# Expert stage of a product-key layer: scatter before the hidden products, weighting on GpSimd, output matmuls three pairs behind

## The reference, cut to what matters

```
for each head h:
    s1, s2   = scores of the query of (t, h) with two sets of 64 keys
    v1, i1   = the 16 best of s1;   v2, i2 = the 16 best of s2
    scores   = the 16 best of all v1[a] + v2[b], with expert = i1[a] * 64 + i2[b]
for each chosen expert e, with its score w:
    hidden   = gelu(expert_down[e] . xn[t]) * relu(w)
    out[t]  += hidden * expert_up[e]
```

## Time and profile before

| | |
|---|---|
| median of 3 runs | 2386.52 us (2382.08 to 2389.36) |
| span of the profiled execution, first to last instruction | 2389.1 us |
| expert loop in it, from the first hidden matmul to the last addition to x | 633.1 to 1861.4 us |
| TensorE, VectorE, ScalarE, GpSimd busy, of the span | 79%, 70%, 28%, 19% |

### The profile page before, as it was taken

The page is one execution under the profiler, slowest core; times in us unless marked ns, Lnnn a source line. Parts: engine busy times, 40 slices in busy tenths (PEclk is TensorE's granted clock), DMA queues, the critical chain, the costliest instruction groups (busy, mean ns, idle before and its releaser), DMA issues. The chain is left out here.

```text
span 2389.1 us, 47903 instructions
## 1 busy us (share of the span) xinstructions
PE 1889.5 (79%) x17539; PEld 1539.2 (64%) x17539; DVE 1684.3 (70%) x6987; ACT 669.6 (28%) x1493; POOL 462.3 (19%) x667
## 2 busy tenths in 40 slices
PE   6595899996479788797787977978769699747995
PEld 3364688874468677686676866767658577544653
DVE  3433666645899999999999999999996477430112
ACT  1342355544222131121311213112120255421220
POOL 2002344330020201202112021120220311021111
PEclk8796899998789899898998988989888799858997
DMA  2232444413400000000000000000000233212434
GB/s 60 70 97 59 113 104 106 99 34 113 102 6 5 2 6 1 6 6 1 6 2 6 5 2 6 1 6 2 1 2 1 60 86 83 68 68 82 141 103 122
DMA packets 90420, 110.24 MB, mean 46 GB/s; under 512 B 27168, under 2 KB 79088, under 8 KB 89552
## 3 DMA queue, kind: packets, MB, share of 16 engines
q1 hardware_dynamic: 84672, 99.09, 15.8%
q0 software_dynamic: 3344, 6.53, 0.8%
q10 hardware_dynamic: 2176, 1.61, 0.2%
HBM read 69.84 MB, written 33.83 MB: 43 GB/s over the span
## 5 line engine op out<-in xcount | busy, mean ns | idle before, releaser
L1665 PE MATMUL peer_out_ps<-peer_g,peer_up 128*128 128x256 f32 (+1 forms) x1664 | 379.0, 393 | 85.1 <-issue 77.1
L1665 PEld LDWEIGHTS peer_out_ps<-peer_g,peer_up 128*128 128x128 f32 x1664 | 326.7, 203 | 133.8 <-issue 85.2
L1630 PE MATMUL peer_x_ps<-peer_xc,peer_dt 128*128 128x256 f32 (+1 forms) x1664 | 352.7, 373 | 19.6 <-DMA peer_up<-in_L_ffn_expert_up_dram 19.5
L1630 PEld LDWEIGHTS peer_x_ps<-peer_xc,peer_dt 128*128 128x128 f32 x1664 | 306.8, 191 | 60.3 <-issue 20.6
L1579 POOL TENSOR_TENSOR peer_g<-peer_g,peer_qt 128x512 f32<-128x512 f32 x96 | 153.0, 1636 | 796.0 <-ACT peer_qt L1790 796.0
L1768 ACT ACTIVATE peer_g<-peer_x_ps 128x512 f32<-128x512 f32 (+1 forms) x208 | 119.1, 573 | 637.1 <-PE peer_x_ps L1630 637.0
L1284 DVE TENSOR_REDUCE l_attn_mx<-l_attn_s_ps 98x4 f32<-98x392 f32 (+1 forms) x320 | 175.0, 560 | 142.7 <-PE l_attn_s_ps L1054 101.6
L1654 PE MATMUL peer_x_ps<-peer_oh_h,peer_oh_a 128*128 128x32 bf16 x3136 | 171.5, 181 | 111.2 <-DVE peer_oh_l L1995 95.6
L1654 PEld LDWEIGHTS peer_x_ps<-peer_oh_h,peer_oh_a 128*128 128x128 bf16 x3136 | 165.1, 99 | 128.5 <-DVE peer_oh_l L1995 63.5
L1988 DVE TENSOR_TENSOR peer_oh_a<-peer_a_t,peer_iota_f 128x8192 bf16<-128x8192 bf16 x49 | 216.6, 4421 | 1.3
L1205 ACT ACTIVATE l_attn_pt<-l_attn_st_ps 98x392 f32<-98x392 f32 x320 | 148.2, 492 | 147.1 <-PE l_attn_st_ps L1067 146.0
(11 more groups left out here) (325 smaller groups left out, 3460.4 us busy)
## 6 DMA issues: line engine op xcount, KB each, us to landing
moe_w<-in_L_ffn_w_dram SPq DMA_DIRECT2D x16, 1024.0 KB, 7.8
l_attn_pieces_q_dram<-l_attn_pieces_q SPq DMA_DIRECT2D x16, 294.0 KB, 3.9
l_attn_pieces_k_dram<-l_attn_pieces_k SPq DMA_DIRECT2D x16, 294.0 KB, 3.2
l_attn_stq<-l_attn_pieces_q_dram SPq DMA_DIRECT2D x16, 294.0 KB
l_attn_stk<-l_attn_pieces_k_dram SPq DMA_DIRECT2D x16, 294.0 KB
peer_g<-n_L_ffn_expert_down_dram SPq DMA_DIRECT2D x8, 512.0 KB
peer_up<-in_L_ffn_expert_up_dram SPq DMA_DIRECT2D x2, 2048.0 KB, 17.6
moe_expert_in<-l_blank SPq DMA_DIRECT2D x16, 197.5 KB
```

Of the source, the lines that this page charges most:

```text
L1630: mm = nc.tensor.matmul(x_ps[b][:, jj * CT:jj * CT + cols], dt[:, k, 2 * jp + jj, :], xc[p][:, k, 0:cols], start=(k == 0), stop=(k == KC - 1))
L1665: mm = nc.tensor.matmul(out_ps[:, m * CT:m * CT + cols], up[:, j, m * P:(m + 1) * P], g[:, j, 0:cols], start=(j == 0), stop=(j == J - 1))
```

## The change

The weights are scattered first, straight into `g`: ScalarE copies each quarter from PSUM to `g` (`scattered`). Only after all scatters of a chunk come the hidden pairs. ScalarE's gelu goes to `act_out`, two buffers in the place of `qt`, and GpSimd multiplies each pair into `g` (`weigh`). TensorE issues the output matmuls of a pair (`pair_out`) three pairs (LAG) after its hidden pair, and the turns of the next chunk after output pair 13 (TURN_AT). GpSimd runs `candidates` of the next chunk after its multiplies 5 and 11 and `index_steps` after the last. VectorE's multiplies are gone, and its addition to `x` of the chunk before (`add_out`, one instruction for each half of the features) stands behind the first one-hots. The second half of the output sums has moved to the bank of `sim_ps[1]`, so `queries` waits for the addition. One of the four halvings in `fold` adds neighbours in place of halves.

```diff
@@ -1398,7 +1397,7 @@
         qt = S.sb("qt", [P, 4, CT])
-        m_copy = [qt[:, 2 * p:2 * p + 2, :].rearrange("p m t -> p (m t)") for p in range(2)]
+        act_out = [qt[:, 2 * p:2 * p + 2, :] for p in range(2)]
         sc = [S.sb(f"sc{p}", [TT, G16, NK]) for p in range(NTILE)]
@@ -1427,14 +1426,15 @@
         sim_ps = [S.ps(f"sim{p}") for p in range(2)]
-        tr_ps, out_ps = S.ps("tr"), S.ps("out")
+        tr_ps = S.ps("tr")
+        out_ps = [S.ps("out"), sim_ps[1]]
@@ -1459,7 +1459,8 @@
         NPAIR = J // 2
-        EARLY = 10
+        LAG = 3
+        TURN_AT = NPAIR - 3
         JS = 8
@@ -1562,24 +1563,25 @@

-            def next_tables(n, tiles):
-
-                for t in range(len(tiles)):
-                    candidates(n, t)
-                index_steps(n)
-
-            next_tables(0, tile_rows(CT))
+            def weigh(n, jp, cols):
+
+                pool.wait_ge(gelu_done, NPAIR * n + jp + 1)
+                pair = g[:, 2 * jp:2 * jp + 2, 0:cols]
+                nc.gpsimd.tensor_tensor(pair, pair, act_out[jp % 2][:, :, 0:cols], ALU.mult).then_inc(g_done, 1)
+
+            for t in range(NTILE):
+                candidates(0, t)
+            index_steps(0)

             def chunk(n, p, now, then):
-
-                for hb in range(LATE, now // HT):
-                    for q in range(4):
-                        pool.wait_ge(m_copied, 4 * (NHB - LATE) * n + 4 * (hb - LATE) + q + 1)
-                        ts = slice(hb * HT + q * GT, hb * HT + (q + 1) * GT)
-                        nc.gpsimd.tensor_tensor(g[:, :, ts], g[:, :, ts], m_copy[q % 2].rearrange("p (t j) -> p j t", j=J),
-                                                ALU.mult).then_inc(g_done_late, 1)
+                tables = dict(zip((5, 11), range(len(tile_rows(then)))))
+                pool.wait_ge(m_copied, 4 * NHB * n + 4 * (now // HT))
+                for jp in range(NPAIR):
+                    weigh(n, jp, now)
+                    if jp in tables:
+                        candidates(n + 1, tables[jp])
                 if then > 0:
-                    next_tables(n + 1, tile_rows(then))
+                    index_steps(n + 1)
             chunks(pool, chunk)
@@ -1603,6 +1605,7 @@
                 wait(pe, sim_ready, NTILE * n)
+                wait(pe, x_done, n - 1)
                 for m in range(4):
@@ -1618,18 +1621,17 @@

-            def hidden(n, p, pairs, cols):
...
+            def hidden(n, p, jp, cols):
+                b = jp % 4
+                if jp < 4:
+                    pe.wait_ge(m_copied, 4 * NHB * n + 4 * (cols // HT) - 3 + jp)
+                else:
+                    pe.wait_ge(gelu_done, NPAIR * n + jp - 3)
+                for jj in range(2):
+                    for k in range(KC):
+                        mm = nc.tensor.matmul(x_ps[b][:, jj * CT:jj * CT + cols], dt[:, k, 2 * jp + jj, :], xc[p][:, k, 0:cols],
+                                              start=(k == 0), stop=(k == KC - 1))
+                mm.then_inc(h_done, 1)

@@ -1644,27 +1646,23 @@
                     if hb == 0:
-                        pe.wait_ge(gelu_done, NPAIR * (n + 1))
-                    elif hb < LATE + 1:
-                        pe.wait_ge(g_done, 4 * LATE * n + 4 * (hb - 1) + q + 1)
+                        wait(pe, gelu_done, NPAIR * n - 3 + q)
                     else:
-                        pe.wait_ge(m_copied, 4 * (NHB - LATE) * n + 4 * (hb - 1 - LATE) + q + 1)
+                        pe.wait_ge(m_copied, 4 * NHB * n + 4 * (hb - 1) + q + 1)
                     for i in range(GT):
...

-            def experts_out(n, cols):
-                n_hb = cols // HT
-                pe.wait_ge(g_done, 4 * LATE * n + 4 * min(LATE, n_hb))
-                pe.wait_ge(g_done_late, 4 * (NHB - LATE) * n + 4 * max(0, n_hb - LATE))
-                wait(pe, x_done, n)
+            def pair_out(n, jp, cols):
+                pe.wait_ge(g_done, NPAIR * n + jp + 1)
                 for m in range(KC):
-                    for j in range(J):
-                        mm = nc.tensor.matmul(out_ps[:, m * CT:m * CT + cols], up[:, j, m * P:(m + 1) * P], g[:, j, 0:cols],
+                    for j in (2 * jp, 2 * jp + 1):
+                        mm = nc.tensor.matmul(out_ps[m][:, 0:cols], up[:, j, m * P:(m + 1) * P], g[:, j, 0:cols],
                                               start=(j == 0), stop=(j == J - 1))
-                mm.then_inc(out_done, 1)
+                if jp == NPAIR - 1:
+                    mm.then_inc(out_done, 1)

@@ -1700,11 +1698,10 @@

+            for t in range(NTILE):
+                turn(0, t, TT)
+
             def chunk(n, p, now, then):
-                hidden(n, p, range(EARLY), now)
-                for t, rows in enumerate(tile_rows(now)):
-                    turn(n, t, rows)
-                hidden(n, p, range(EARLY, NPAIR), now)
                 next_rows = tile_rows(then)
@@ -1712,7 +1709,15 @@
                         scores(n + 1, hb - 1, next_rows[hb - 1])
-                experts_out(n, now)
+                wait(pe, x_done, n)
+                for jp in range(NPAIR + LAG):
+                    if jp < NPAIR:
+                        hidden(n, p, jp, now)
+                    if jp >= LAG:
+                        pair_out(n, jp - LAG, now)
+                    if jp - LAG == TURN_AT:
+                        for t, rows in enumerate(next_rows):
+                            turn(n + 1, t, rows)
             chunks(pe, chunk)
@@ -1762,32 +1767,44 @@

-            def hidden_out(n, pairs, cols):
-                for jp in pairs:
+            def scattered(n, hb):
+                for q in range(4):
+                    act.wait_ge(m_done, 4 * NHB * n + 4 * hb + q + 1)
+                    ts = slice(hb * HT + q * GT, hb * HT + (q + 1) * GT)
+                    nc.scalar.activation(g[:, :, ts], x_ps[q][:, 0:GT * J].rearrange("p (t j) -> p j t", j=J), ACT.Copy).then_inc(m_copied, 1)
+
+            def hidden_out(n, cols):
+                for jp in range(NPAIR):
                     act.wait_ge(h_done, NPAIR * n + jp + 1)
-                    nc.scalar.activation(g[:, 2 * jp:2 * jp + 2, 0:cols], x_ps[jp % 4][:, 0:2 * CT].rearrange("p (j t) -> p j t", j=2)[:, :, 0:cols],
+                    wait(act, g_done, NPAIR * n + jp - 1)
+                    nc.scalar.activation(act_out[jp % 2][:, :, 0:cols], x_ps[jp % 4][:, 0:2 * CT].rearrange("p (j t) -> p j t", j=2)[:, :, 0:cols],
                                          ACT.Gelu).then_inc(gelu_done, 1)

+            def turned(n, t, rows):
+                act.wait_ge(tr_done, NTILE * n + t + 1)
+                ts = slice(t * TT, t * TT + rows)
+                if t == 0:
+                    wait(act, oh_ready, NHB * n)
+                for dst, c in ((wh_t, 2), (a_t, 0), (b_t, 1)):
+                    ins = nc.scalar.activation(dst[:, ts, :], tr_ps[:, c * TT:c * TT + rows].unsqueeze(2).broadcast_to([P, rows, R]), ACT.Copy)
+                ins.then_inc(tr_ready, 1)
+
+            for t in range(NTILE):
+                turned(0, t, TT)
+
             def chunk(n, p, now, then):
+                next_rows = tile_rows(then)
                 wait(act, out_done, n)
-                hidden_out(n, range(EARLY), now)
...
+                for hb in range(now // HT):
+                    scattered(n, hb)
+                    if hb == 0 and then > 0:
+                        wait(act, g_done, NPAIR * n)
+                        query_out(n + 1, then)
+                    if 0 < hb <= len(next_rows):
+                        score_out(n + 1, hb - 1, next_rows[hb - 1])
+                hidden_out(n, now)
+                for t, rows in enumerate(next_rows):
+                    turned(n + 1, t, rows)
             chunks(act, chunk)
@@ -1887,6 +1904,9 @@
                     chain.step(nc.vector.tensor_tensor(low, low, high, ALU.add))
+                elif n == H // 4:
+                    pairs = m[:, 0:2 * n, :].rearrange("t (a b) k -> t b a k", b=2)
+                    chain.step(nc.vector.tensor_tensor(m[:, 0:n, :], pairs[:, 0, :, :], pairs[:, 1, :, :], ALU.add))
                 elif n > 1:
@@ -1968,9 +1988,6 @@

...
                 q = hb % 2
@@ -1986,21 +2003,18 @@
                 nc.vector.tensor_tensor(view(oh_a[q]), spread(a_t, P), number(P), ALU.is_equal)
-                weigh_last(0)
                 chain.step(nc.vector.tensor_tensor(view(oh_l[q]), spread(b_t, J), number(J), ALU.is_equal))
-                weigh_last(1)
                 chain.wait()
                 nc.vector.tensor_tensor(view(oh_h[q]), view(oh_l[q]), spread(wh_t, J), ALU.mult)
-                weigh_last(2)
                 nc.vector.tensor_tensor(view(oh_l[q]), view(oh_l[q]), spread(wl_t, J), ALU.mult).then_inc(oh_ready, 1)
-                weigh_last(3)
-
-            def weigh(n, hb, q):
...
+            def add_out(n, cols):
+
+                dve.wait_ge(out_done, n + 1)
+                for m in range(KC):
```

(44 more changed lines are left out.)

18 lines of the change are left out of this document (1 added, 17 removed).

## The result

| | median | lowest to highest | against the kernel before |
|---|---|---|---|
| before | 2387.02 us, 4 runs | 2382.08 to 2389.36 | |
| after | 2488.51 us, 4 runs | 2483.14 to 2493.16 | 1.0431 [1.0409, 1.0452] |

The median rose by 101.5 us; the forecast was +84.5. The profiled execution is the fastest of the four: its span of 2481.4 us is 92.3 above that of before, and the expert loop ends 94.9 us later, at 1956.35 against 1861.42.

The account below looks back on a forecast made before the run. Bound before: the order of work, neither VectorE nor TensorE alone; after: a chain through GpSimd. Start -4.6, eleven periods +60.5, last steady one +14.9, tail +13.7, total +84.5 on 2386.5: 2471 us, range 2455 to 2512.

Parts of the forecast that it names:

- The chain through GpSimd: Hidden pair 15, its multiply, `index_steps`, rest of `make_codes`, turn, copies: period 104.5 us in place of 99.0; chance 0.72.
- One sign that the prediction named: VectorE's longest wait stands before the first product of `make_codes`, released by GpSimd's step copies.
- inside the 10.6: VectorE loses 10.6 us a chunk at `times_steps`; its stop for the second tile's `candidates` lies inside that.
- the 48.4 us for 28 pairs at 1.73: TensorE, after the last scatter: sixteen hidden and twelve output pairs at 1.73 us take 48.4 us.
- slow-clock rival: TensorE begins each pair phase at 1.2 GHz: 2.7 us lost twelve times, 32 us more, 2503 us; chance 0.14.
- the slower fold: The regrouped halving in `fold` at half speed: 0.3 us twice a chunk, 7 us in all; with collisions, chance 0.05.
- Eleven periods: Chunk 0 to chunk 11 of the expert loop: 11 x 5.5 = +60.5 us.
- Chunk 11 to the tail: Last full chunk to the tail chunk: 104.5 us against 89.6, the new chain not getting shorter: +14.9 us.
- the tail: Tail chunk: hidden and output pairs now come after its scatter, 41.5 us against 27.75: +13.7 us.
- The start: First turn no longer behind ten hidden pairs: chunk 0 begins at 650.5 against 655.08, -4.6 us.
- Collisions: GpSimd multiplies beside VectorE: taken as nothing; other end 11 us, 2482 us; with a slower fold, chance 0.05.
- VectorE as the bound: Rival: steps come by 79.5 us, VectorE's loop is 94.0, 46 us saved, 2340 us; chance 0.06.

Follow-up runs that it names:

- e1: Kernel before, with GpSimd's index steps made to wait for the seventh early hidden pair of the next chunk: 2538.28 us, 1.0661.
- e3: Changed kernel with LAG = 12 in place of 3, GpSimd's order untouched: 2342.22 us, 0.986; run once more, 2337.06 us, 0.9812.
- e5: Changed kernel with LAG = 6 in place of 3, nothing else: 2416.16 us, 1.0121.
- e9: Changed kernel with LAG = 9 in place of 3: 2372.74 us, 0.9934.
- e2: Changed kernel with `candidates` after multiplies 4 and 8 and `index_steps` at once behind the second: 2387.97 us, 1.0009.
- e4: Changed kernel with only `index_steps` moved, to right behind the second `candidates` (after multiply 11): 2435.71 us, 1.021.
- e7: Kernel of e2 with multiplies 12 to 15 cut to one column, every wait kept: 2338.47 us, 0.9793.
- e6: Changed kernel with five unused matmuls on TensorE ahead of the fourth scatter: 2478.36 us, 1.0382.

## Why the prediction was right

**The mechanism.** The chain through GpSimd sets the period. e1 shows the wait alone is enough; e3, e5 and e9 show that the time falls as fewer output pairs stand ahead of the last hidden pair, with nothing else touched; e2 and e4 show which two table steps on GpSimd carry it. One sign that the prediction named did not come as written: the longest wait of a steady chunk stands ahead of the second tile's maxima (7.4 us, released by `candidates`), and the one before `times_steps` is 2.2. The prediction had the `candidates` stop "inside the 10.6" without a size; it is the larger part. The 13 us ahead of the turn came as named (13.05).

**VectorE's period can be added up.** This is bookkeeping on one engine, and shows where the time stands, not why; the causes are shown by the experiments above. e3 is VectorE's loop without a stop: 93.55 us over eleven periods (T0 654.55 and 1683.65); the prediction had 94.0 for that case. What the others take beyond it is their stops a chunk (totals of the view of waits, without chunk 11 where that stands out), the longer turn (2.68 against 2.33 in the rows) and the lengthened rows:

| kernel | stop for `candidates` | stop for the steps | turn, beyond e3's | lengthened rows | sum with 93.55 | period measured |
|---|---|---|---|---|---|---|
| after (LAG 3) | 7.29 | 2.20 | 0.35 | 0.96 + 1.07 | 105.4 | 105.5 |
| e4 | 6.39 | 0 | 0.35 | 0.96 + 1.06 | 102.3 | 102.3 |
| e5 (LAG 6) | 1.83 | 2.22 | 0.35 | 0.96 + 1.06 | 100.0 | 100.1 |
| e2 | 0 | 0 | 0.35 | 4.17 | 98.1 | 98.0 |
| e9 (LAG 9) | 0 | 0.31 | 0.35 | 2.35 | 96.6 | 96.4 |
| e7 | 0 | 0 | 0 | 0 | 93.6 | 93.6 |

**The chain, term by term,** in the chunk shown, in us after its T0 and with the prediction's count in brackets: fourth build done 33.5 (33.7), last scatter done 37.2 (37.2), gelu 15 begins 86.7 (85.6), multiply 15 done 88.6 (87.8), steps there 91.1 (90.1), codes done 103.1 (102.0), first copy 104.2 (102.9), next T0 105.8 (104.5). The term that was mis-sized is the 48.4 us for 28 pairs at 1.73: every pair but the first holds to it (a hidden and an output pair follow each other in 3.45), and the first is 1.2 late in this chunk, 1.0 in the mean of chunks 0 to 10. That is a part of the slow-clock rival, which had 2.7; e6 shows its cause. The multiply was cheaper (1.27 to 1.36 against 1.54), the turn dearer (1.08 against 0.9, at a granted clock of 0.50 behind TensorE's idle 13 us), `index_steps` 2.5 against 2.3. The regrouped halving of `fold` (L1909) takes 0.42 to 0.43 us, as the one of 512 elements did before (0.42 to 0.43), so the slower fold is out. The Trainium skill (TensorE: Matmul & The Clock Gate, HAM oscillation) says that bursts parted by long waits each begin at the lower rate; here the turn began so, at 0.50; the scatter ahead of pair 0 began at 1.00 and the clock fell inside it, so that only the pair behind it was slow.

**The sum.** Eleven periods gave +71.5 (forecast +60.5): the 1.0 us above, eleven times, is all that was missed there. Chunk 11 to the tail gave +15.1 (+14.9), the tail +13.9 (+13.7). The start gave -5.5 (-4.6), but this term can't be called shown: in e2, e3, e4 and e9, which have the same program up to there, T0 of chunk 0 lies anywhere from 645.20 to 655.32, and before it was 655.08. Together +95.0 at the end of the loop. The two medians lie further apart, 101.5 against 92.3 for the spans, because after's span lies 7.1 below the median of its runs and before's 2.1 above. The forecast is 17.5 us short of the median: 10.4 of it stand in the expert loop, and most of the rest is this choice of executions; where after's other runs lose their 1 to 10 us isn't seen.

**Collisions.** The prediction took nothing for them, as the multiplies run beside searches of maxima. That held for the searches: `MAX8` and `FIND_INDEX8` keep their lengths beside a multiply (0.22, and 0.21 to 0.23 us). Two of the code arithmetic's instructions did meet multiplies 14 and 15 (L1946 and L1951, 2.03 us), one more than expected. They lie ahead of the stop for the steps, so in the changed kernel they cost nothing: without them the stop would by estimate be 2.17 + 2.03 = 4.2 us. So the nothing in the sum came out, but in part by luck: not because nothing collides, which was its reason, but because a stop follows. They become a price as soon as the stop goes: 4.17 us a chunk in e2. The Trainium skill (SBUF — State Buffer, Who interferes with whom) says that a VectorE instruction with two SBUF inputs and a GpSimd instruction that reads SBUF shut each other out, and that `tensor_scalar` can meet the same lock in some of its modes; L1951 and L1946 agree, each ending 0.2 to 0.3 us behind the multiply beside it.

**The rival on the other side.** VectorE as the bound was put at 2340, if the pair phase ended six pairs earlier. With exactly six fewer (e9) the stop was gone, as said, but the tables then fell on VectorE's arithmetic, and it took nine (e3) to reach 2342 and 2337.
